# Four heads' causal maxima from one burst of 32-row products, read from the projections' staging, with the stacking cut into four transfers each

## What is computed

```python
q = jnp.einsum('btc,hcd->bhtd', xn, Wq) + bq[None, :, None, :]
k = jnp.einsum('bsc,hcd->bhsd', kv_src, Wk) + bk[None, :, None, :]
v = jnp.einsum('bsc,hcd->bhsd', kv_src, Wv) + bv[None, :, None, :]
scale = DH ** (-0.5)
scores = jnp.einsum('bhtd,bhsd->bhts', q, k) / scale
if causal:
    scores = jnp.where(mask[None, None], scores, -jnp.inf)
attn = jax.nn.softmax(scores, axis=-1)
```

## Time and profile before

| | |
|---|---|
| median of three runs | 2273.32 us |
| the profiled execution's own time | 2272.72 us |
| its span, first to last instruction | 2270.9 us |
| TensorE busy | 2161.4 us, 95% |
| VectorE, GpSimd, ScalarE busy | 1395.7, 932.4, 868.7 us |
| granted TensorE clock, mean | 0.984 |

### The profile page before, as it was taken

How to read it: one execution, slowest core, us unless ns; L and a number is a source line. 1 busy time by engine, 2 the same in 40 slices (tenths; PEclk the granted TensorE clock), 3 DMA queues, 4 the chain that set the end, 5 groups by cost and what they waited for, 6 DMA issues and landing times.

```text
span 2270.9 us, 32174 instructions
## 1 busy us (share of the span) xinstructions
PE 2161.4 (95%) x11590; PEld 1604.5 (71%) x11590; DVE 1395.7 (61%) x3349; ACT 868.7 (38%) x1610; POOL 932.4 (41%) x943
## 2 busy tenths in 40 slices
PE   7999999999999998889999998999999999999996
PEld 5666666666656664467777776888887887888784
DVE  5577766876786676456666677543455636455546
ACT  4156555655565555534333433221221222121213
POOL 1068767777777778643333342101020202111112
PEclk9999999999999997999999999999999999999998
DMA  7655555555564564211122121320112121121101
GB/s 234 78 82 97 93 85 87 106 89 83 91 111 76 82 96 126 71 56 56 56 70 77 63 80 42 121 84 24 61 61 82 53 74 66 65 66 56 42 33 47
DMA packets 106324, 177.34 MB, mean 78 GB/s; under 512 B 18335, under 2 KB 23455, under 8 KB 106161
## 3 DMA queue, kind: packets, MB, share of 16 engines
q1 hardware_dynamic: 106164, 175.29, 33.1%
HBM read 83.67 MB, written 40.13 MB: 55 GB/s over the span
## 4 chain that ended last, share of the span: by engine, by line
PE 81%; DVE 7%; ACT 5%; issue 3%; POOL 2%; DMA 1%; SPq 0%; POOLq 0%; ACTq 0%; DVEq 0%
PE psum L55 19%; PE psum L56 18%; PE psum L57 18%; PE psum L821 6%; PE psum L766 6%; PE psum L809 5%; PE psum L724 1%; DVE psum L1027 1%; ACT sx L1377 1%; PE psum L830 1%; PE psum L743 1%; PE psum L1327 1%; DMA small<-es 1%; PE psum L1319 1%; PE psum L1268 1%
## 5 line engine op out<-in xcount | busy, mean ns | idle before, releaser
L681 POOL TENSOR_TENSOR es<-es,er 128x512 f32<-128x512 f32 (+3 forms) x640 | 588.0, 959 | 258.4 <-PE psum L821 243.6
L922 ACT ACTIVATE er<-psum 128x512 f32<-128x512 f32 (+3 forms) x640 | 278.4, 471 | 285.6 <-DVE psum L1038 176.2
L1027 DVE CUSTOM_DVE_ANT_0 psum<-psum,mask_ts 128x384 f32<-128x384 f32 (+3 forms) x512 | 249.4, 502 | 152.9 <-PE psum L766 150.6
L766 PE MATMUL psum<-ks,qs 96*128 96x512 f32 (+3 forms) x768 | 260.4, 371 | 7.4 <-DVE mx L1027 3.5
L809 PE MATMUL psum<-qs,ks 100*128 100x512 f32 (+3 forms) x768 | 252.0, 365 | 10.6 <-DVE mx L1027 5.1
L1876 ACT ACTIVATE fy<-psum,cols 128x512 f32<-128x512 f32 x128 | 88.2, 689 | 451.9 <-PE psum L57 451.4
L766 PEld LDWEIGHTS psum<-ks,qs 96*128 96x128 f32 x768 | 139.7, 191 | 115.2 <-issue 32.9
L1031 DVE TENSOR_REDUCE mx<-psum 128x1 fp32r<-128x512 f32 x256 | 175.6, 686 | 61.0 <-PE psum L766 60.0
L55 PE MATMUL psum<-fh,hh 128*128 128x512 f32 x512 | 201.0, 393 | 7.1 <-DVE hl L1977 7.1
L55 PE MATMUL psum<-fah,fh 128*128 128x512 f32 x512 | 202.9, 396 | 0.0
L1975 DVE CAST hh<-fy 128x512 fp32r<-128x512 f32 x128 | 61.2, 478 | 228.5 <-ACT fy L1876 228.1
(11 more groups left out here) (260 smaller groups left out, 4588.7 us busy)
## 6 DMA issues: line engine op xcount, KB each, us to landing
qs<-stage SPq DMA_DIRECT2D x96, 256.0 KB, 5.7
ks<-stage SPq DMA_DIRECT2D x96, 256.0 KB, 8.3
rs<-rs_d SPq DMA_DIRECT2D x32, 256.0 KB
sa_d<-rs SPq DMA_DIRECT2D x32, 256.0 KB, 2.1
sx<-sa_d SPq DMA_DIRECT2D x8, 1024.0 KB, 5.7
xt<-in_x SPq DMA_DIRECT2D x32, 256.0 KB, 6.0
x_d<-xt SPq DMA_DIRECT2D x32, 256.0 KB, 2.0
fw<-in_Wf SPq DMA_DIRECT2D x16, 512.0 KB, 5.3
```

The lines of the kernel that those rows point to most:

```text
L681: e.tensor_tensor(es, es, er, ALU.add).then_inc(s_add.sem, 1)
L766: t = e.matmul(bank1(*s)[:, v * wd:v * wd + wd], Q.qs[par][0:96, i, 128 * ti:128 * ti + 128], Q.ks[par][0:96, i, c0:c0 + wd], start=True, ...
L922: e.activation(dst, bank1("sc", g, c2, j, i)[:, off:512], ACT.Exp, scale=SCALE).then_inc(s_freeS.sem, 1)
L1027: t = e.tensor_tensor_reduce(out=ps, in0=ps, in1=mask_ts[:, 512 - wd:512], scale=1.0, scalar=-3e38, op0=ALU.add, op1=ALU.max, accum_out=mx ...
```

## The change

The maxima no longer read the stacked tiles. A new step `mb` takes one unit of 128 queries and up to 512 keys for four heads: four products of 32 rows each, head h from rows 32h to 32h + 31 of `stage[0]` (q, high half) and `stage[2]` (k, high half), into four different banks. The low halves no longer take part in the maxima: the number that is taken off before the exponential comes from high times high alone. There are 12 such units per group and 192 in all; VectorE's reductions stay as many and as wide as before (all of one head now: 48 per group). TensorE waits for all four banks before the first product, and a reduction waits for the fourth product of its unit. In the order an `mb` stands `MAX_LEAD` = 0.008 of a group ahead of the first of its four reductions, which stay spread out.

The host no longer interleaves Wq and Wk: a head is 32 neighbouring rows of `stage`. So a `stack` step becomes 12 transfers of 64 KB, 32 partitions into 32 partitions. `pjh` waits in addition until the maxima of group g - 1 that read the same part of `stage` are through. The constants of the order are new: `MAX` of the middle groups runs from -0.97 to about -0.20, the projections of a group go from -1.335 to about -1.06 (before: -1.95 to -1.06), and `CROSS_AT` and its fellows shift by up to a tenth of a group, a few by more.

```diff
-MAXU = []
-for _ti in range(8):
...
+MAXU = [(ti, 0, min(512, 128 * ti + 128), ti < 4) for ti in range(8)]
+MAXU += [(ti, 512, 128 * ti - 384, True) for ti in range(4, 8)]
...
-MAX = ((-1.031, -0.726, -0.051), (-1.012, -0.739, -0.002), (-1.033, -0.705, -0.043), (-0.988, -0.72, -0.05))
+MAX_LEAD = 0.008
+MAX_0 = 0.033
...
+        maxima = spread(m0, m1, max_steps(g, 0)) + spread(m1, end, max_steps(g, 1))
+        t += maxima + [(a - MAX_LEAD, ("mb", g, s[2] // 4)) for a, s in maxima if s[0] == "mx" and s[2] % 4 == 0]
...
                     for r, part in enumerate(((0, 1, 0), (0, 0, 1))[wq]):
-                        e.dma_start((Q.qs, Q.ks)[wq][par][32 * r:32 * r + 32, :, ts].bitcast(F32),
-                                    Q.stage[2 * wq + part][:, ts].bitcast(F32)).then_inc(stk(par, wq, c2).sem, 16)
+                        for h in range(4):
+                            e.dma_start((Q.qs, Q.ks)[wq][par][32 * r:32 * r + 32, h, ts].bitcast(F32),
+                                        Q.stage[2 * wq + part][32 * h:32 * h + 32, ts].bitcast(F32)).then_inc(stk(par, wq, c2).sem, 16)
...
-                elif s[0] == "mx":
...
+                elif s[0] == "mb":
+                    _, g, u = s
+                    ti, c0, wd, diag = MAXU[u]
+                    w.wait_ge(s_hi, 4 * g + 2 * (ti // 4) + 1)
+                    w.wait_ge(s_hi, 4 * g + 2 * (c0 // 512) + 2)
+                    for h in range(4):
+                        free1(w, "mx", g, 4 * u + h)
+                    for h in range(4):
+                        rows = slice(32 * h, 32 * h + 32)
+                        e.matmul(bank1("mx", g, 4 * u + h)[:, 0:wd], Q.stage[0][rows, 128 * ti:128 * ti + 128],
+                                 Q.stage[2][rows, c0:c0 + wd], start=True, stop=True).then_inc(s_fillM.sem, 1)
...
                     if g:
-                        w.wait_ge(stk((g - 1) % 2, wq, c2), 48 * ((g - 1) // 2 + 1))
+                        w.wait_ge(stk((g - 1) % 2, wq, c2), 192 * ((g - 1) // 2 + 1))
+                        w.wait_ge(s_fillM, Q.useM["mx", g - 1, 15 if (c2, wq) == (0, 0) else 47] + 1)
...
-    stacked = lambda w: w.reshape(-1, 4, 4, 32).transpose(0, 1, 3, 2).reshape(-1, 512)
...
-    for n in "qk":
-        lay[f"W{n}_s"] = stacked(lay[f"W{n}_s"])
-        lay[f"b{n}_s"] = stacked(lay[f"b{n}_s"])
```

More of the change, by code:

```diff
@@ L57, in three @@
     return e.matmul(dst, ll, rh, start=False, stop=stop)
-MAXU = []
-for _ti in range(8):
-    _wd = 128 * (_ti + 1)
-    _per = 4 if _ti == 0 else 2 if _ti == 1 else 1
-    for _h0 in range(0, 4, _per):
-        for _c0 in range(0, _wd, 512):
-            _w = min(512, _wd - _c0)
-            MAXU.append((_ti, _h0, _per, _c0, _w, _c0 + _w == _wd))
-NMAX0 = sum(u[0] < 4 for u in MAXU)
+MAXU = [(ti, 0, min(512, 128 * ti + 128), ti < 4) for ti in range(8)]
+MAXU += [(ti, 512, 128 * ti - 384, True) for ti in range(4, 8)]
 def spread(start, end, steps):
@@ L100, in max_steps @@
 def max_steps(g, c2):
-    for r, (ti, h0, per, c0, w, diag) in enumerate(MAXU):
+    for u, (ti, c0, w, diag) in enumerate(MAXU):
         if ti // 4 == c2:
-            yield ("mx", g, r), per * w + 100
+            for h in range(4):
+                yield ("mx", g, 4 * u + h), w + 100
     if c2:
@@ L158, in order1 @@
         for qt in range(4):
-            t += ln_times(b, qt, 4 * b + LN_LOAD[qt], 4 * b + LN_TURN[qt])
+            t += ln_times(b, qt, 4 * b + LN_LOAD[b - 1][qt], 4 * b + LN_TURN[b - 1][qt])
     for g in range(16):
-        r = g % 4
+        r = row(g)
         cut = CUT[r]
-        at = [at0(a) for a in PROJ_0] if g == 0 else [g + a for a in (PROJ_1 if g == 1 else PROJ[r])]
+        at = [at0(a) for a in PROJ_0] if g == 0 else [g + a for a in PROJ[r]]
         for c2 in range(2):
@@ L221, in banks1 @@
         use = s[:2] if s[0] == "wb" else s[:3] if s[0] == "vm" else s[:4] if s[0] == "pj" else s
-        if use in ends and use not in bank:
-            b = min((k for k in range(7) if ends[use] < until.get(k, 99)), key=lambda k: free[k])
-            bank[use], before[use], last[b], free[b] = b, last.get(b), use, ends[use]
-    return bank, before, last
-CROSS_AT = 16.793
-CROSS_LOAD = (14.019, 14.431, 14.754, 14.309, 15.318)
-CROSS_SPLIT = (14.581, 14.853, 15.576)
-CROSS_ONCE = (14.168, 15.027, 14.983, 15.099, 14.261, 15.089, 15.146, 14.946)
-CROSS_KEYS = (15.173, 15.19, 15.199, 15.461, 15.405)
-CROSS_0 = (15.723, 15.776, 15.812, 16.19)
+        burst = [("mx", s[1], 4 * s[2] + h) for h in range(4)] if s[0] == "mb" else [use]
+        taken = []
+        for use in burst:
+            if use in ends and use not in bank:
+                b = min((k for k in range(7) if ends[use] < until.get(k, 99) and k not in taken), key=lambda k: free[k])
+                bank[use], before[use], last[b], free[b] = b, last.get(b), use, ends[use]
+                taken.append(b)
+    return bank, before, last
+CROSS_AT = 16.699
+CROSS_LOAD = (13.988, 14.515, 14.902, 14.417, 15.272)
+CROSS_SPLIT = (14.676, 14.854, 15.577)
+CROSS_ONCE = (14.303, 15.057, 15.013, 15.119, 15.0, 15.119, 15.176, 15.06)
+CROSS_KEYS = (15.112, 15.129, 15.138, 15.4, 15.344)
+CROSS_0 = (15.834, 15.792, 15.828, 16.179)
 def order2():
@@ L444, in program @@
                 Q.useP[s[:4]] = len(Q.useP)
-            if s[0] in ("mx", "mxT"):
-                Q.useM[s] = len(Q.useM)
+            if s[0] == "mb":
+                fills += 4
+                Q.useM.update({("mx", s[1], 4 * s[2] + h): fills - 1 for h in range(4)})
+            if s[0] == "mxT":
+                Q.useM[s], fills = fills, fills + 1
             if s[0] in ("sc", "fin"):
@@ L1016, in dve1 @@
                     _, g, r = s
-                    ti, h0, per, c0, wd, diag = MAXU[r]
+                    (ti, c0, wd, diag), h0 = MAXU[r // 4], r % 4
                     u, mx = Q.useM[s], Q.mx[:, g % 2, :]
@@ L1024, in dve1 @@
                     if diag:
-                        for v in range(per):
-                            ps = bank1(*s)[:, v * wd:v * wd + wd]
-                            t = e.tensor_tensor_reduce(out=ps, in0=ps, in1=mask_ts[:, 512 - wd:512], scale=1.0, scalar=-3e38,
-                                                       op0=ALU.add, op1=ALU.max, accum_out=mx[:, at + v:at + v + 1])
-                        t.then_inc(s_red.sem, 1)
+                        ps = bank1(*s)[:, 0:wd]
+                        e.tensor_tensor_reduce(out=ps, in0=ps, in1=mask_ts[:, 512 - wd:512], scale=1.0, scalar=-3e38,
+                                               op0=ALU.add, op1=ALU.max, accum_out=mx[:, at:at + 1]).then_inc(s_red.sem, 1)
                     else:
@@ L1112, in stacked @@
             for lane in d_stk.values():
[L1113 removed]
+                w.wait_ge(lane, 192 * 8)
+            w.wait_ge(s_fillM, Q.useM["mx", 15, 47] + 1)
         def max_done(w):
[L1117 removed]
+            w.wait_ge(s_red, 48 * 16)
             w.wait_ge(s_tq, 32)
```

63 lines of the change are left out of this document (26 added, 37 removed).

## The result

The changed kernel takes **2438.64 us** (median of four runs, 2416.68 to 2441.68) against 2272.61 for the kernel before on the same chip (four runs): **1.0708 times as long, 95% interval 1.066 to 1.0757**, or 166 us more. The forecast was 2256 us and the range ended at 2306, so the sign and the range were wrong. The profiled execution after took 2441.03 us.

A forecast was written before the change was run, and what follows sets the result against it. TensorE was taken to bound the self-attention, with VectorE and GpSimd a quarter to spare. From 2272.7 us, 26.4 saved on TensorE and 9.6 added for bank waits gave 2255.9, stated as 2256 us; range 2220 to 2306.

The forecast's parts named there:

- The four banks: Self-attention bursts waiting for four of seven banks: 0.05 us added wait each, 9.6 us in all; bounds -0.24 to 0.69.
- the bound of -0.24: Best case per burst in the bank term: today's 45.2 us of waits for reductions, spread over 192 bursts, gone.
- The order: Self-attention maxima in 0.78 of a group instead of 0.96, projections with no room: costed at nothing, VectorE's spare time as cover.
- SyncE: Stacking queue, 192 transfers becoming 768: 0.33 us per issue, cost zero; at 0.60 us per issue, 32 us.
- The clock: Granted clock: no change taken, said of the self-attention stage's tail, with 10 us kept on either side.
- TensorE's saving: Self-attention maxima on TensorE: 136.3 us before, 109.9 after as row-quarter bursts with shape changes, so 26.4 us saved.
- the first pass: Column-quarter products with the values: first pass of four takes 0.45 us, so four row quarters also run at once.
- Rival 4: Row quarters in the bursts don't overlap: streaming stays 136.3 us, shape changes add 72, giving 2345 us; chance 0.05.
- The tail: End of the self-attention stage and cross-attention's first steps, partly at half clock: no change, 10 us on either side.
- Rival 2: Bursts wait for the last of four reductions: at half a reduction, 0.34 us each, 65 us, giving 2311 us; chance 0.27.

The follow-up runs named there:

- e14: e8 with each burst of four products and four banks cut into two bursts of two products and two banks: 2335.07 us, ratio 1.0273.
- e11: The kernel before with only its maxima squeezed to end at -0.20 of a group, from g = 2 on: 2284.42 us, ratio 1.0044.
- e12: The kernel before with projections from the fifth group on packed as closely as the changed kernel's, and later than its own: 2287.2 us, ratio 1.0069.
- e8: e6 plus bursts: four heads' 96-row products into four banks, units in the changed kernel's order, no row quarters, three transfers: 2427.14 us, ratio 1.0703.
- e1: The changed kernel with three stacking transfers of 128 partitions in place of twelve (heads mixed, scores scaled by 1/256): 2390.94 us, ratio 1.0508.
- e9: e4 with every reduction of the maxima over 128 columns only, scores scaled by 1/256: 2367.55 us, ratio 1.0395.
- e7: e4 with a burst's four reductions close together in VectorE's order and a gap behind the fourth: 2383.44 us, ratio 1.0507.
- e6: The kernel before with only the changed kernel's order constants; single 96-row products from the stacked tiles, three transfers: 2351.66 us, ratio 1.0351.
- e2: The kernel before with only the twelve transfers per stack step and the host order that belongs to them: 2322.16 us, ratio 1.0209.
- e3: The changed kernel with each burst product over all 128 rows of `stage`, so no row quarters (scores scaled by 1/256): 2424.27 us, ratio 1.0663.
- e17: e7 with each burst of four row quarters cut into two bursts of two heads and two banks: 2424.16 us, ratio 1.0686.
- e4: The changed kernel with each stack step cut into four steps of three transfers, 0.045 of a group apart: 2396.07 us, ratio 1.0542.

## Why the prediction was wrong

As a chain of steps by their medians, each of one or a few edits: before 2272; **+63** for order and pairs of banks (e14, 2335; e11 and e12 have 11 and 17 of it alone); **+92** for four banks at once in place of two (e8, 2427); **-36** for row quarters read from `stage` (e1, 2391); **+48** for twelve transfers (2439).

1. **The four banks: the failed step.** The prediction took 0.05 us a burst, "near zero, because the reductions keep their places in VectorE's order and VectorE has 23 to 31% idle". From two banks to four it is 92 / 192 = 0.48 us a burst, inside the bounds given (up to 0.69) but more than three times the 0.14 from which it decides. VectorE's idle share was no cover: e9 made the reductions short and the loss stayed; each still came at its place in the order. Nor were today's waits there to be won back, the bound of -0.24: the earlier trace rows hold loads and products together, and 40.7 of the 45.2 us are loads that waited while products ran; the products stood for 4.5 us. The reading that fits is that a burst needs four of seven banks at one moment, and all that shares them (scores, projections, `mxT`) waits in TensorE's order behind it. That it is the number at one moment and not the longer holding of each bank is argued, not shown: e14 changes both, and e7, which shortens the holding, gave 13 us at most. Of the waits named before bursts, only part is for reductions (126.8 us); the exponentials that free a bank (49.2 us) and "issue" (65.1 us) grow with them. How the 92 us divide among these and the clock (point 4) wasn't settled.
2. **The order: costed at nothing.** One set of `stage` for maxima and projections forces late, packed projections and early maxima. The prediction saw it ("no room") and still took VectorE's spare time as the cover. Measured: 11 us for the maxima, 17 for the projections, each alone, 63 with all constants and pairs; 79 with the old order of units (e6), where the transfers of k come late. The 35 us between 63 and the two parts were not taken apart.
3. **SyncE: the wrong row.** I took 0.33 from the copy into memory (L628), since "the new ones are plain". It is 0.59, what the reshaping transfer took the earlier trace rows. The other end given was 32 us; it is 48 (e1) to 49 (e2). The working (24 issues in a row, the sums behind them, the reciprocal waiting) was right; it counted VectorE's wait alone, while ScalarE's exponentials wait for the same transfer (32.4 us) and the loads of x stand behind it too (17.3 us).
4. **The clock: also costed at nothing.** "I take no change" was said of the tail, and stage 1 had no term for it. It is 371 us at the lower level in place of 73. e3 has 145 and is 14 us faster with some 30 us more work by the prediction's prices. What the lower level costs can be estimated, since the executions of one kernel differ in it by themselves. After took 2416.68 us with 304 us of it and 2441.68 with 381; e8 took 2423.92 with 199 and 2446.80 with 269; e17 took 2417.27 with 328 and 2442.75 with 395. That is 0.32 to 0.38 us of time for each us at the lower level. At 0.32 the 298 us more are some 95 of the 166 us. They lie inside the steps of the chain and not beside them: about 19, 27, 32 and 21 us of the +63, +92, -36 and +48. This is an estimate, and time and clock may share a cause. Waits are not the only thing that the clock falls with: from 100 to 900 us e17 has TensorE 96% busy and a clock of 0.85, e14 has 95% and 0.98. Why it falls with row quarters stays open.
5. **TensorE's saving: the first pass right, the sum not settled.** 26.4 us were forecast. e8 to e1 measures 36, with intervals of about 11 us on either side, and it contains the change of source. But e3 to after, where only the rows of the products change, measures 14 us the other way. Both contain the lower clock that came with the row quarters, by the estimate above 32 us in the first. So the nearness of 36 to 26.4 is in part luck: a larger saving less a cost that the prediction did not have. The burst's own times (0.26, 0.32, 0.38 to the next start) are in keeping with 0.45 for the first pass of four. Rival 4 (no overlap) is out. The 92 us saved that an estimate from the Trainium skill gave (TensorE: Matmul & The Clock Gate, Part 3) are in no pair of runs here; the bursts stand alone and pay for their changes of shape.
6. **The tail: right.** Stage 2 and 3 last as long as before.

Rival 2 had the place and the kind of wait, at half a reduction a burst, and a chance of 0.27. It was priced at 65 us, with nothing beside it; the other costs came on top. The warning that it cited (TensorEngine Tiling, Performance Considerations, in the Trainium skill), that tiling doesn't speed up the emptying of PSUM, is borne out in kind: 126.8 us of waits for reductions in place of 45.2. What the runs add is that the emptying need not be slow for it: VectorE was busy for 60 and 63% of the two stretches shown.

## What to carry to other kernels

Count how many buffers one instruction group needs at the same moment, as a share of all, and not only how busy the engine is that empties them: going from two of seven banks to four cost 0.48 us each time here. (What two cost against one was not measured by itself.) When a change needs a new order, time the order alone with the old instructions first. And split long rows of transfers on a queue that also carries something that others wait for: the same 48 issues a group cost 48 us in all in rows of 12 to 24 and about 5 in threes (e4 against e1, with intervals of some 12). Last, give the granted clock a line in the sum: waits and row quarters both came with a lower one here, and by the estimate in point 4 that is more than half of the loss.

## What the runs showed of the hardware

- A transfer from one on-chip tile to another took the same time to issue with 32 partitions and 64 KB (0.590 us) as with 128 and 256 KB (0.603), though it landed in 2.0 us in place of 5.7 and 8.3 us. Between these two the issue's price did not follow the size; the copy to memory took 0.326 before and 0.431 after.
- Four row quarters with 32 rows each run at once (0.45 us for four of 384 columns, the next product 0.38 after the first start), and the granted clock is lower with them: 0.924 against 0.970 for the same bursts over 128 rows (e3), and 0.945 to 0.959 for four 96-row products (e8). From 100 to 900 us, with TensorE 96 and 95% busy, pairs of row quarters have 0.85 (e17) and pairs of 96-row products 0.98 (e14).
- Executions of the same kernel that had more time at the lower level took longer, by 0.32 to 0.38 us for each us of it in after, e8 and e17. No run changed the clock alone.
